# Attention and feed-forward block on one core: the bias row's split behind the first head, the first row of maxima in front of the last value store

## The reference

```python
x = L0_attn_query                                   # [2, 2048, 512]
mod = (silu(c) @ wmod)                              # six rows per batch: shifts, scales, gains
h = layernorm(x) * (1 + ca) + sa
# attention: 2 x 16 heads of 32, 2048 queries by 2048 keys
q, k, v = h @ Wqkv.T                                # split by head
attn = softmax(q @ k.T / sqrt(32))
out = (attn @ v) @ Wproj.T + bproj                  # the bias row, 512 numbers
x = x + ga * out
h = layernorm(x) * (1 + cb) + sb
hidden = fwht(silu(h @ W1.T) * (h @ W3.T))
x = x + gb * (hidden @ W2.T)
```

## Time and profile before

| what | us |
|---|---|
| median of 3 runs | 3136.89 |
| lowest and highest | 3132.02, 3137.76 |
| the profiled execution | 3138.33 |
| its span in the trace | 3136.5 |
| PE busy | 3077.2 (98%) |
| DVE, ACT, POOL busy | 1878.3, 1516.8, 1418.8 |
| last value store issued by SP | 374.54 |
| first instruction of the attention on PE | 378.73 |
| bias row copied by ACT | 389.81 |
| first exponential | 391.75 |
| end of head 31's exponentials, near | 1933 |

### The profile page before, as it was taken

The page is one execution under the profiler, slowest core; times in us unless marked ns, Lnnn a source line. Parts: engine busy times, 40 slices in busy tenths (PEclk is TensorE's granted clock), DMA queues, the critical chain, the costliest instruction groups (busy, mean ns, idle before and its releaser), DMA issues. The chain is left out here.

```text
span 3136.5 us, 41501 instructions
## 1 busy us (share of the span) xinstructions
PE 3077.2 (98%) x15564; PEld 2103.1 (67%) x15564; DVE 1878.3 (60%) x3184; ACT 1516.8 (48%) x2852; POOL 1418.8 (45%) x489
## 2 busy tenths in 40 slices
PE   6999899999999999999999999999999999999998
PEld 4777655555555555555555554778888888888887
DVE  4444788888888888888888882743332323323232
ACT  3333176666666666666666666543222222222221
POOL 2223088888888888888888885000000000000000
PEclk8999999999999999999999999999999999999999
DMA  6666568888888888888888875762211112111111
GB/s 236 188 193 203 145 128 174 182 181 174 186 182 175 182 181 183 177 182 180 184 180 179 178 162 147 256 217 81 88 44 61 61 48 71 45 60 61 47 57 34
DMA packets 148776, 446.40 MB, mean 142 GB/s; under 512 B 26849, under 2 KB 44513, under 8 KB 113378
## 3 DMA queue, kind: packets, MB, share of 16 engines
q0 software_dynamic: 28592, 204.48, 31.6%
q1 hardware_dynamic: 118930, 239.25, 25.8%
q10 hardware_dynamic: 1056, 0.00, 0.0%
HBM read 166.85 MB, written 80.21 MB: 79 GB/s over the span
## 5 line engine op out<-in xcount | busy, mean ns | idle before, releaser
L1211 DVE TENSOR_REDUCE mxp<-pmax 128x1 f32<-128x512 f32 x1968 | 1202.8, 680 | 245.0 <-PE pmax L987 244.8
L1158 ACT ACTIVATE prob<-pexp 128x512 f32<-128x512 f32 x2023 | 1021.2, 624 | 403.1 <-PE pexp L1036 399.8
L987 PE MATMUL pmax<-k,q 96*128 96x512 f32 x1968 | 813.3, 413 | 4.6 <-PEq L429 4.6
L1036 PE MATMUL pexp<-q,k 98*128 98x512 f32 x2023 | 805.7, 400 | 10.6 <-ACT prob L1158 9.9
L51 PE MATMUL pproj<-h2f,w 128*128 128x512 f32 x3072 | 717.5, 389 | 0.0
L51 PEld LDWEIGHTS pproj<-h2f,w 128*128 128x128 f32 x3072 | 576.5, 188 | 119.7 <-issue 0.3
L1288 POOL TENSOR_TENSOR gsum<-gsum,prob 128x2048 f32<-128x2048 f32 x127 | 583.6, 4595 | 37.3 <-ACT prob L1158 27.8
L987 PEld LDWEIGHTS pmax<-k,q 96*128 96x128 f32 x1968 | 375.0, 191 | 284.1 <-DVE mxp L1211 169.2
L1047 PE MATMUL pctx<-prob,v 128*32 128x512 f32 x4096 | 496.5, 601 | 0.0
L1288 POOL TENSOR_TENSOR gsum<-prob 128x2048 f32<-128x2048 f32 x96 | 458.7, 4778 | 44.3 <-ACT prob L1158 44.2
L1036 PEld LDWEIGHTS pexp<-q,k 98*128 98x128 f32 x2023 | 382.8, 190 | 136.0 <-ACT prob L1158 21.7
(11 more groups left out here) (134 smaller groups left out, 1659.6 us busy)
## 6 DMA issues: line engine op xcount, KB each, us to landing
gsum<-prob POOLq DMA_DIRECT2D x187, 1024.0 KB, 7.4
w<-w_scratch SPq DMA_DIRECT2D x128, 256.0 KB, 2.6
q<-q_scratch SPq DMA_DIRECT2D x96, 256.0 KB, 4.4
k<-k_scratch SPq DMA_DIRECT2D x96, 256.0 KB, 6.2
q_scratch<-obq SPq DMA_DIRECT2D x32, 512.0 KB, 5.1
k_scratch<-obq SPq DMA_DIRECT2D x32, 512.0 KB, 3.7
xin<-in_L_attn_query_dram SPq DMA_DIRECT2D x8, 1024.0 KB, 9.3
v_scratch<-vst SPq DMA_DIRECT2D x8, 1024.0 KB, 5.8
```

Source lines behind the costliest of these rows:

```text
L987: pe.matmul(pmax[:, bank, :], qst[slot][0:KR, qt * P:(qt + 1) * P], kst[slot][0:KR, kc * TOK:(kc + 1) * TOK], start=True, stop=True).then_ ...
L1036: pe.matmul(score_bank(g, n), kst[slot_of(g)][:, kt * P:(kt + 1) * P], qst[slot_of(g)][:, j * TOK:(j + 1) * TOK], start=True, stop=True).t ...
L1158: act.activation(prob_tile(g, kt)[:, j * TOK:(j + 1) * TOK], score_bank(g, n), ACT.Exp, scale=SCALE).then_inc(exp_done, 1)
L1211: dve.tensor_reduce(mxp[:, par, u // QJ, u % QJ:u % QJ + 1], pmax[:, bank, :], X, ALU.max).then_inc(mx_done, 1)
```

## The change

Three edits. The last tile's `store` returns before its value store; that store (the same transfer, now in a function `store_values`) becomes SP's first instruction in `attend`, so that `send_max_row` for head 0 follows the key stores of the last tile at once. `vst` is handed on for it. On ACT the wait for the bias row and its copy move from the front of `attend` behind `step(0)`; on DVE the wait for the copy and the subtraction do the same. No operation is added or taken out.

```diff
+def store_values(sp, scratch, vst, v_out, t):
+
+    b, s = t // ST, t % ST
+    sp.dma_start(scratch["v"][b * NH:(b + 1) * NH, :, bass.ds(s * TK * HD, TK * HD)].rearrange("g p n -> p g n"),
+                 vst[:, t % 2, :, :, :].rearrange("p h k d -> p h (k d)")).then_inc(v_out[t % 2], 16)
...
-        vst = sb("vst", [P, 2, NH, TK, HD])
+        vst = keep["vst"] = sb("vst", [P, 2, NH, TK, HD])
...
+                    if t == TILES - 1:
+                        return
                     sp.wait_ge(out_hi, NJ * (t + 1))
-                    sp.dma_start(scratch["v"][b * NH:(b + 1) * NH, :, bass.ds(s * TK * HD, TK * HD)].rearrange(
-                        "g p n -> p g n"), vst[:, t % 2, :, :, :].rearrange("p h k d -> p h (k d)")
-                                 ).then_inc(v_out[t % 2], 16)
+                    store_values(sp, scratch, vst, v_out, t)
...
+                store_values(sp, scratch, keep["vst"], v_out, TILES - 1)
                 load_values(0, 0)
...
-                act.wait_ge(bias_in, 16)
-                act.activation(bias[0:1, :], braw[:, :], ACT.Copy).then_inc(bias_hi, 1)
                 for g in range(LAST):
                     step(g)
+                    if g == 0:
+                        act.wait_ge(bias_in, 16)
+                        act.activation(bias[0:1, :], braw[:, :], ACT.Copy).then_inc(bias_hi, 1)
...
-                dve.wait_ge(bias_hi, 1)
-                dve.tensor_tensor(blow[:, :], braw[:, :], bias[0:1, :], ALU.subtract).then_inc(bias_lo, 1)
-                heads(step)
+                for g in range(HEADS):
+                    step(g)
+                    if g == 0:
+                        dve.wait_ge(bias_hi, 1)
+                        dve.tensor_tensor(blow[:, :], braw[:, :], bias[0:1, :], ALU.subtract).then_inc(bias_lo, 1)
```

## The result

The changed kernel took 3115.24 us in the median of four runs (3114.97 to 3117.38), the kernel before 3136.02 (3132.02 to 3137.76): ratio 0.9936, 95% interval 0.992 to 0.9952, or 20.8 us less. Forecast were 3120.0 us (16.9 less) and a range of 3115.0 to 3126.5, so the time lies inside it, 0.24 us above its low end. The profiled execution took 3115.38 us with a span of 3113.6; its lines are numbered anew (L995 is the old L987, L1044 the old L1036, L1166 the old L1158, L1220 the old L1211, L1055 the old L1047, L1312 and L1329 the carry and the merge, L1270 the split).

A forecast was written before the change was run, and what follows sets the result against it. PE (98% busy) was taken as the bound, its attention start held up by the bias row. Border 3.5, bias row 11.8 and clock 1.6 made 16.9 us off the 3136.89 median: 3120.0 us, range 3115 to 3126.5.

The forecast's parts named there:

- The border: Between projection and attention: attention begins at 375.18 instead of 378.7, 3.5 us gained.
- The table load ahead of the wait: ACT's start in the attention: exponential table loads before scores arrive, 375.18 to 376.46, so exponential 0 starts at 376.5.
- The clock: PE at the border stands still only 1.1 us and keeps its higher clock through exponentials 0 to 7: 1.6 us.
- rival A: PE's clock falls at the border all the same: gain 15.1 us, 3121.8; chance 0.10.
- The sum at exponential 8: Second block of head 0: exponential 8 starts at 380.6 instead of 397.50, 16.9 us gained.
- Passing it on: Steady state behind head 0: everyone waits for PE, so the rest of the attention shifts by the same amount.
- The value load and the store: Start of attention: value load lands by 383.4, before first weighing at 384.0; store holds POOL up to 0.2 us; hidden.
- The copy and the split behind head 0: Border of heads 0 and 1: copy (0.63 us) and split (0.68 us) fit idle gaps of ACT and DVE; no cost.
- B: Border of heads 0 and 1: split caught behind POOL's merge, PE stands 4.2 us; gain 12.7, 3124.2; chance 0.15.
- C: Start of attention: value load stuck behind all loads, PE waits 5.8 us at first weighing; gain 11.1, 3125.8; chance 0.05.
- D: Later heads: POOL's shifted start makes 29 divisions take 4.53 us instead of 0.68; 62 us slower, 3199; chance 0.03.
- E: First exponentials find another wait of the old length; only the border's 3.5 us remain, 3133.4; chance 0.05.

The follow-up runs named there:

- split on POOL: Changed kernel with the bias row's subtraction done by POOL behind its first head, none on DVE: 3117.15 us, 17.1 less than before.
- delay: Changed kernel with six small DVE memsets between the wait for the copy and the split: 3117.57 us median, one of five runs at 3124.48.
- store behind the loads: Changed kernel with the last value store issued behind all the first loads of the attention: 3125.96 us.
- bias row alone: Against the kernel before, only the bias row's copy and split move behind head 0; store and row of maxima stay: 3132.17 us, 3.6 less.
- split inside an addition: Changed kernel with DVE's split moved into head 1 behind its 16th reduction, 0.2 us into a POOL addition: 3124.17 us.
- second comparison: Changed kernel run again unaltered against the kernel before: 3118.45 us against 3135.74, 17.3 less.
- row of maxima alone: Against the kernel before, only store and row of maxima change places; bias row still copied first: 3137.1 us against 3135.74, ratio 1.0002.

## Why the prediction was right

**The border, 3.5 us:** right (0.34 us from DVE's end to PE's start, 0.32 forecast). **The table load ahead of the wait:** right; exponential 0 came 1.60 us after the last DVE instruction, forecast 1.64. By the 2.66 us with drain of the Trainium skill, ScalarE: Activation LUTs, What ACT_TABLE_LOAD costs, it would have been 3.0, an estimate; no drain shows in the earlier trace rows nor here. **The clock, 1.6 us:** it stayed up in the changed kernel's two traces and in three of the four further traces in which the exponentials follow the short border at once (split on POOL, delay, store behind the loads; the fourth is under rival A), and the eight exponentials took 3.82 us, a little less than the full pace of 4.12, with no wait for PE among them. **The sum at exponential 8:** 17.2 local against 16.9. **Passing it on:** right, 17.0 to 17.3 us through 29 heads.

**The value load and the store:** hidden, as said. PE has no wait at the first weighing, which came 8.84 us after the last DVE instruction, forecast 9.1. POOL was held by the store for longer than I had allowed (it began at 378.61, 1.10 us after exponential 7's end; before it was 0.53, not the 0.3 of the prediction, so the store held it 0.6 us, where I had 0.2), and its idle time took that in.

**The copy and the split behind head 0:** right for the changed kernel, 0.61 us in ACT's gap and a split of 0.68 us that began 0.45 us ahead of the merge's recorded start (forecast 0.24) and ended 0.23 us behind it. But part of this was luck. Nothing in the prediction's rows told a free split from a caught one at this distance. In the nine runs of the changed kernel (none above 3118.98) no time says that it was caught. With the same distances to within some hundredths of a microsecond the split was caught in one of five runs of the delayed kernel, and in the kernel with the bias row alone the trace shows it caught and all eleven runs (3129.81 to 3134.18) lie above what it takes without (3122.09 to 3124.24, in the other group, whose kernel before is 1.5 us faster). And B's price was mis-sized: 4.2 us forecast, 6.3 to 7.2 measured. The term that was missing is the clock, which fell behind the stops of 3.03 and 3.87 us; the trace of before shows such a fall, and I had used it at the border and not here. With B the gain would have been 10, not 12.7.

**Rival A** turned up in one trace (split inside an addition) at 1.3 us, forecast 1.8. **C, D and E** didn't occur; 29 of DVE's 32 operations of this kind (31 divisions and the split) took 0.68 us in the changed kernel as before.

**The number:** the median lies 4.8 us below the forecast. 0.3 of it is the sum; the rest is most likely scatter of the kind for which the low end had been set, and that it stopped 0.24 us short of that end is luck: in the second comparison the medians stand 17.3 apart and in a third, with the split on POOL, 17.1. The traces show two places of it, the first two programs (the last DVE instruction ends anywhere from 371.5 to 374.9) and head 30 (44.7 to 48.0 us). For head 30 that is not shown: it took 44.7 us in both traces of the changed kernel.

**Are the parts worth their sum?** No: the bias row alone gives 3.6 us as written, 10.8 without the catch; the row of maxima alone -0.2 us by the traces; both together 17.2. The second edit removes a wait that stood in front of a later one, and pays only once the bias row is out of the way.

## What to carry to other kernels

Before moving a small instruction into a gap, ask what the next instruction of another engine shares with it, and price a loss of that race with everything that a stalled PE loses, its clock included. If the gap is won by tenths of a microsecond, give the work to the other engine itself, if that has idle time (here the subtraction on POOL took 1.3 us that nobody waited for). And an edit that is worth nothing alone can be worth a third of the gain together with another: look at what is late next, after both.

## What the runs showed of the hardware

A DVE subtraction of two SBUF tensors on a single partition, 0.68 us long, took 4.99, 5.78 and 5.83 us beside a POOL operation of 4.6 to 4.8 us and ended some 0.55 us behind it. The number of partitions made no difference: in the ten traces 30 divisions of 128 x 512 began 0.35 to 4.17 us inside a POOL addition, and each ended 0.55 or 0.56 us behind it. The subtraction was caught even though it began 0.40 and 0.46 us ahead of that operation's recorded start, and was not caught in other traces that began 0.45 and 0.46 us ahead of it. The recorded lead doesn't decide: in the trace with the store behind the loads the split began only 0.19 us ahead of an addition, was free, and the addition took 5.30 us:

```profile
422.34 0.67 DVE L1270 TENSOR_TENSOR blow<-braw,bias 1x512 fp32r<-1x512 f32 x1
...
422.52 5.30 POOL L1299 TENSOR_TENSOR gsum<-gsum,prob 128x2048 f32<-128x2048 f32 x1
```

Nor does POOL's idle time before its transfer, which was 1.23 us in the changed kernel (free) and 1.23 in the delayed one (caught), 1.60 in the one with the bias row alone (caught). The transfer that POOL issues before the merge was recorded 0.15 to 0.16 us ahead of the split in both traces of the changed kernel (free) and in the one with the bias row alone (caught), so that doesn't tell them apart either. What decides stays open. The GPSIMD Engine Reference of the Trainium skill (8. Key points) names the shared interfaces; the traces agree with it for each operation that began inside a POOL addition.

PE's granted clock fell to the lower level behind the stops of PE named here (4.61 us at the old border, 3.03, 3.87 and 3.87 us behind caught splits, 2.14 and 4.44 us with the store behind the loads). It fell also in one of the six traces with a stop of only 1.1 us between two stretches of work, some 3 us after PE had stopped and 2 us after it had started again.
